# Graph network, edge stage: single node rows fetched by SyncE and ScalarE, and store addresses loaded in pairs

## The reference, cut to what matters

```python
N, C, E = 12500, 64, 412500              # nodes, channels, edges (sorted by dst)
def message_layer(x, e, nvec, src, dst):
    x_send, x_recv = x[src], x[dst]      # one row of the node table for each edge
    flux_send = einsum('ecd,ed->ec', mlp_flux(x_send).reshape(E, C, 2), nvec)
    flux_recv = einsum('ecd,ed->ec', mlp_flux(x_recv).reshape(E, C, 2), nvec)
    a_ws = mlp_a((x_send + x_recv) * 0.5)         # 3 hidden layers of 64, layer norm
    flux = 0.5 * (flux_send + flux_recv) - 0.5 * a_ws * (x_send - x_recv)
    return x + segment_sum(flux, dst, N)
x = layernorm(x + three_mean_aggregations(x, src, dst))
return layernorm(x + message_layer(x, edge_attr_64, edge_attr_2, src, dst))
```

## Time and profile before

| | |
|---|---|
| three runs, median | 7139.81 us (7138.31 to 7141.95) |
| the profiled execution: its time, its span | 7138.85 us, 7137.1 us |
| edge stage: first gather to last | 3056.9 to 7072.0 us |
| busy over the span: PE, DVE, ACT, POOL | 76%, 68%, 37%, 72% |
| gathers of the edge stage | 3199 of 0.951 us, mean |

### The profile page before, as it was taken

The page is one execution under the profiler, slowest core; times in us unless marked ns, Lnnn a source line. Parts: engine busy times, 40 slices in busy tenths (PEclk is TensorE's granted clock), DMA queues, the critical chain, the costliest instruction groups (busy, mean ns, idle before and its releaser), DMA issues.

```text
span 7137.1 us, 176662 instructions
## 1 busy us (share of the span) xinstructions
PE 5406.3 (76%) x49929; PEld 4402.1 (62%) x50131; DVE 4861.2 (68%) x9655; ACT 2628.9 (37%) x5446; POOL 5165.2 (72%) x5041
## 2 busy tenths in 40 slices
PE   2699999999999999946666666666666666666665
PEld 2599999999999999934444444444444444444443
DVE  6899898933223555566777777777777777777776
ACT  0588888920000111123333333333333333333333
POOL 4588887847775777367777777777777777777774
PEclk6799999999999999978888888888888888888887
DMA  5333333446666777656666666666666666666664
GB/s 159 119 139 139 138 138 127 143 169 227 226 227 214 244 238 242 204 153 160 173 166 170 165 170 169 168 168 169 170 165 170 169 171 165 170 166 173 165 170 116
DMA packets 578142, 1230.55 MB, mean 172 GB/s; under 512 B 335288, under 2 KB 416189, under 8 KB 550923
## 3 DMA queue, kind: packets, MB, share of 16 engines
q0 software_dynamic: 211504, 615.59, 32.4%
q1 hardware_dynamic: 316622, 568.88, 24.0%
q10 hardware_dynamic: 49405, 38.76, 1.9%
HBM read 1020.92 MB, written 197.70 MB: 171 GB/s over the span
## 4 chain that ended last, share of the span: by engine, by line
POOL 21%; issue 13%; PE 8%; DMA 6%; SPq 6%; ACT 1%; ACTq 1%; DVE 0%; POOLq 0%; DVEq 0%
POOL edge_rows L1978 21%; DMA edge_rows<-node_table,edge_et 5%; PE edge_mp L2006 4%; SPq L1891 2%; SPq L1888 2%; PE edge_zp L2017 1%; PE edge_tp L1995 1%; SPq L1835 1%; PE edge_tp L1998 1%; ACT edge_h L2082 1%; DMA node_sums<-edge_seg 1%; PE edge_sums_ps L2032 1%; SPq L1923 1%; ACTq L1835 0%; DMA edge_et<-edges_turned 0%
## 5 line engine op out<-in xcount | busy, mean ns | idle before, releaser
L1978 POOL DMA_INDIRECT edge_rows<-node_table,edge_et x3199 | 3041.1, 951 | 975.4 <-issue 923.3
L1995 PE MATMUL edge_tp<-ident,edge_yc 128*128 128x128 f32 x1612 | 539.7, 354 | 1384.2 <-ACT edge_h L2082 1344.5
L1386 PE MATMUL two_acc<-x_parts,win 128*128 128x192 bf16 x16072 | 1387.8, 247 | 17.2 <-issue 11.2
L874 POOL DMA_INDIRECT two_rows<-x_parts,src_at x1120 | 1063.8, 950 | 449.7 <-issue 340.0
L1386 PEld LDWEIGHTS two_acc<-x_parts,win 128*128 128x128 fp8e4 x16072 | 1344.2, 98 | 28.8 <-issue 18.2
L2074 ACT ACTIVATE edge_yc<-edge_rows 128x512 f32<-128x512 f32 x403 | 253.7, 630 | 2571.6 <-DMA edge_rows<-node_table,edge_et 2521.5
L1995 PEld LDWEIGHTS edge_tp<-ident,edge_yc 128*128 128x128 f32 x1612 | 283.9, 176 | 1474.9 <-issue 1407.9
L2006 PE MATMUL edge_mp<-edge_h,edge_W 128*128 128x512 f32 x1612 | 1159.8, 860 | 8.9 <-ACT edge_h L2082 8.9
L1106 ACT ACTIVATE win<-one_count 128x784 fp8e4<-128x784 f32 x1312 | 1071.2, 825 | 144.6 <-PE one_count L1057 80.9
L874 POOL DMA_INDIRECT one_rows<-x_parts,src_at x560 | 862.4, 1540 | 181.7 <-issue 169.4
L2221 DVE TENSOR_REDUCE edge_ssq<-edge_sq 128x8 f32<-128x512 f32 x403 | 276.3, 686 | 959.7 <-ACT edge_sq L2089 953.8
(11 more groups left out here) (334 smaller groups left out, 7475.5 us busy)
## 6 DMA issues: line engine op xcount, KB each, us to landing
win<-adjacency SPq DMA_DIRECT2D x80, 3136.0 KB
adjacency<-win SPq DMA_DIRECT2D x41, 3136.0 KB
edge_near<-near_ids SPq DMA_DIRECT2D x101, 768.0 KB
edge_lone_rows<-node_table SPq DMA_DIRECT2D x3200, 1.3 KB
edge_rows<-node_table,edge_et POOLq DMA_INDIRECT x3199
two_rows<-x_parts,src_at POOLq DMA_INDIRECT x1120
node_table<-two_row SPq DMA_DIRECT2D x49, 322.0 KB
edge_own<-node_table SPq DMA_DIRECT2D x46, 322.0 KB
```

The lines of the kernel that those rows point to most:

```text
L874: pool.indirect_dma_start(rows[:, b % ring, e, :], None, XP.rearrange("p (j c) -> (p j) c", c=3 * C), bass.IndirectOffsetOnAxis(ap=src_at[ ...
L1386: mm = pe.matmul(acc[b][:, half * 3 * C:(half + 1) * 3 * C], win[:, b, half, j, :].bitcast(FP8), now[:, j, :], start=(j == 0), stop=(j == ...
L1978: pool.indirect_dma_start(rows[:, h.b, t, :], None, T5, bass.IndirectOffsetOnAxis(ap=et[:, h.b, 0, t:t + 1].bitcast(I32), axis=0))\
L1995: pe.matmul(to, yc[:, h.b % 2, 2 * pr:2 * pr + 2, :].rearrange("p t c -> p (t c)"), ident[:, :], is_transpose=True, start=True, stop=False)
```

## The change

SP fetches a lone tile in every eight steps instead of every sixteen: tile 0 of the steps 10, 18, ... 402, 50 in all (`LONES`). ACT fetches one more in every sixteen steps: tile 0 of the steps 62, 78, ... 398, 22 in all (`ACT_LONES`); it issues 8 rows in each of ten steps and 12 in each of the four after them, and does none in the two left (`ACT_FETCHED`). SP issues 20 rows in four steps and 16 in three (`LONE_FETCHED`), places its own tile in the eighth step, and places ACT's in the fourth step of every second round.

The row addresses are made at the stage's start: SP loads the source numbers of all these tiles, DVE multiplies them by the bytes of a row, SP writes them to a scratch tensor `LONE`, and a tile's list is read from there. Registers are then loaded without a check of bounds (`several`), and the DMA uses the loaded byte address as it is (`fetch_rows`). SP loads the addresses of the `y_parts` windows eight at once, for four steps; ACT loads the two store addresses of a step at once. ACT's loop body becomes sixteen steps long instead of eight.

```diff
-LONE = 2 * RB
-LONE_AT = (HS - 1) % LONE
-LONE_FIRST = LONE_AT + LONE
-LONE_QUEUES = 4
+LONE_AT = (HS - 1) % RB
+LONE_FIRST = LONE_AT + RB
+LONES = (HS - LONE_FIRST + RB - 1) // RB
+LONE_QUEUES = 8
+PEEL = DONE_PEEL + 2 * RB
+ACT_FROM, ACT_TURNS, ACT_AHEAD = DONE_PEEL + RB, 14, 19
+ACT_TARGET = ACT_FROM + ACT_AHEAD
+ACT_LONES = (HS - RB - ACT_FROM) // (2 * RB)
+ACT_FETCHED = tuple(8 * k + 4 * max(0, k - 10) for k in range(ACT_TURNS + 1))
+LONE_FETCHED = (0, 20, 40, 60, 80, 96, 112, P)
...
+        def several(engine, a, most, why):
+            return nc.values_load_multi_w_load_instructions(a, engines=(engine,), min_val=0, max_val=most, skip_runtime_bounds_check_because=why)[1]
+
+        def fetch_rows(eng, engine, mine, at, to, signals):
+
+            begins = several(engine, at[0:1, mine.start:mine.stop], (N - 1) * 4 * W5, "node numbers of the edges' sources")
+            table = T5.rearrange("n c -> (n c)").bitcast(U8)
+            for i, begin in zip(mine, begins):
+                eng.dma_start(row_bytes(to[i:i + 1, :]), table[bass.ds(begin, 4 * W5)].rearrange("(o a c) -> o a c", o=1, a=2))\
+                    .then_inc(signals[i % LONE_QUEUES], 16)
+
+        def store(eng, h, u, at=None):
...
+            at = base_of(eng, 2 * h.c + u) if at is None else at
...
+            sp.wait_ge(lone_scaled, 2)
+            sp.dma_start(LONE[0:LONES, :], lone_bytes[:, :]).then_inc(lone_listed, 16)
+            sp.dma_start(LONE[LONES:LONES + ACT_LONES, :], act_bytes[:, :]).then_inc(lone_listed, 16)
...
-                sp.dma_start(lone_ids[:, :], src[bass.ds((h.c + LONE - 1) * HE, P)].rearrange("(o e) -> o e", o=1)).then_inc(lone_ids_in, 16)
+                sp.dma_start(lone_at[:, :], LONE[bass.ds(n, 1), :]).then_inc(lone_at_in, 16)
...
+                    bases[:] = several(mybir.EngineType.SP, base_i[0:1, bass.ds(2 * h.c, RB)], N - 1, "bases are held at or under the last node")
...
+                if h.place == ACT_TARGET:
+                    place_rows(h, h.twice, act_in, act_rows, act_placed)
-            double_turns(sp, step, HS, DONE_PEEL + 2 * RB)
+            double_turns(sp, step, HS, PEEL)
...
-                lone = h.place % LONE == LONE_AT and not early(h, LONE_FIRST)
-                for t in range(1 if lone else 0, TL):
+                lone, apart = h.place % RB == LONE_AT and not early(h, LONE_FIRST), h.place == ACT_TARGET
+                for t in range(1 if lone or apart else 0, TL):
...
+                    if apart and t == TL - 1:
+                        pool.wait_ge(act_placed, 16 * (h.twice + 2))
+                        pool.sem_inc(sems["issued"], 1)
...
+            def fetch_own(h):
+                turn = h.place - ACT_FROM - 1
...
+                if turn == 0:
+                    act.wait_ge(act_at_in, 16 * (h.twice + 1))
...
+                    act.wait_ge(act_placed, 16 * (h.twice + 1))
...
+                fetch_rows(act, mybir.EngineType.Activation, range(ACT_FETCHED[turn], ACT_FETCHED[turn + 1]), act_at, act_rows, act_in)
...
                 done_root(h)
+                list_rows(h)
+                fetch_own(h)
...
-            chunks(act, step, HS - RB, RB, DONE_LAG)
+            double_turns(act, step, HS - RB, ACT_FROM)
...
+            dve.wait_ge(lone_src_in, 64)
+            dve.tensor_scalar(act_bytes[:, :], act_src[:, :], float(4 * W5), None, ALU.mult).then_inc(lone_scaled, 1)
+            dve.tensor_scalar(lone_bytes[:, :], lone_src[:, :], float(4 * W5), None, ALU.mult).then_inc(lone_scaled, 1)
```

More of the change, by code:

```diff
@@ L1873, in list_lone @@
             def list_lone(h):
[L1875 removed]
+                n = lone_number(h)
+                if early(h, LONE_AT + 2):
+                    sp.wait_ge(lone_listed, 32)
+                    sp.sem_inc(sems["storing"], 1)
+                sp.dma_start(lone_at[:, :], LONE[bass.ds(n, 1), :]).then_inc(lone_at_in, 16)
             def fetch_lone(h, turn):
@@ L1885, in fetch_lone, with place_rows @@
                         sp.sem_inc(sems["storing"], 1)
[L1886 to L1896, removed]
+                fetch_rows(sp, mybir.EngineType.SP, range(LONE_FETCHED[turn], LONE_FETCHED[turn + 1]), lone_at, lone_rows, lone_in)
+            def place_rows(h, n, arrived, fetched_rows, placed):
                 for q in range(LONE_QUEUES):
-                    sp.wait_ge(lone_in[q], 16 * P // LONE_QUEUES * (n + 1))
+                    sp.wait_ge(arrived[q], 16 * P // LONE_QUEUES * (n + 1))
                     sp.sem_inc(sems["storing"], 1)
@@ L1908, in step @@
                     sp.sem_inc(sems["storing"], 1)
-                if lone_turn == 0 and not early(h, LONE_AT + 1):
+                if turn_of_lone == 0 and not early(h, LONE_AT + 1):
                     list_lone(h)
@@ L1921, in step @@
                                  NEAR16[bass.ds(h.c * HE, 4 * HE)].partition_broadcast(WK)).then_inc(near_in[h.b // 4], 16)
+                    bases[:] = several(mybir.EngineType.SP, base_i[0:1, bass.ds(2 * h.c, RB)], N - 1, "bases are held at or under the last node")
+                at_turn = 2 * (h.place % 4)
+                if h.place == PEEL and at_turn:
+                    bases[at_turn:] = several(mybir.EngineType.SP, base_i[0:1, bass.ds(2 * h.c, RB - at_turn)], N - 1, "bases are held at or under the last node")
                 for u in range(2):
-                    sp.dma_start(yd[:, h.b % 4, u, C:2 * C], Y3[bass.ds(base_of(sp, 2 * h.c + u) * 3, WK), :]).then_inc(yd_in[h.b % 4], 16)
+                    own_base = bases[at_turn + u]
+                    sp.dma_start(yd[:, h.b % 4, u, C:2 * C], Y3[bass.ds(own_base * 3, WK), :]).then_inc(yd_in[h.b % 4], 16)
                 if not early(h, DONE_PEEL):
@@ L2106, in take, with list_rows @@
                 act.activation(seg[:, h.b, :], fold_ps, ACT.Copy).then_inc(sems["seg_out"], 1)
+            def list_rows(h):
+                if h.place == ACT_FROM:
+                    act.wait_ge(lone_listed, 32)
+                    act.dma_start(act_at[:, :], LONE[bass.ds(LONES + h.twice, 1), :]).then_inc(act_at_in, 16)
+            def fetch_own(h):
+                turn = h.place - ACT_FROM - 1
+                if turn < 0 or turn >= ACT_TURNS:
+                    return
+                if turn == 0:
+                    act.wait_ge(act_at_in, 16 * (h.twice + 1))
+                    act.sem_inc(sems["issued"], 1)
+                    act.wait_ge(act_placed, 16 * (h.twice + 1))
+                    act.sem_inc(sems["issued"], 1)
+                fetch_rows(act, mybir.EngineType.Activation, range(ACT_FETCHED[turn], ACT_FETCHED[turn + 1]), act_at, act_rows, act_in)
             def step(h):
+                ats = None
                 if not early(h, ACT_BACK):
-                    store(act, h.back(ACT_BACK), 0)
+                    ats = several(mybir.EngineType.Activation, base_i[0:1, bass.ds(2 * h.back(ACT_BACK).c, 2)], N - 1, "bases are held at or under the last node")
+                    store(act, h.back(ACT_BACK), 0, ats[0])
                 take_y(h)
@@ L2115, in step @@
                 if not early(h, ACT_BACK):
-                    store(act, h.back(ACT_BACK), 1)
+                    store(act, h.back(ACT_BACK), 1, ats[1])
                 for k, run in stages[3:]:
```

53 lines of the change are left out of this document (35 added, 18 removed).

## The result

The changed kernel takes 7105.35 us in the median (7091.37 to 7109.55), the kernel before in the same comparison 7140.88. The ratio is 0.9947 with an interval of 0.9931 to 0.9963: 35.5 us faster, where 60 were forecast, and outside the forecast range. The profiled execution took 7109.55 us, its span 7107.8. It is the slowest of four (7091.37, 7104.17, 7106.53, 7109.55), so what is lost differs from one execution to the next, and what follows is read from one trace of each kernel.

A forecast was written before the change was run, and what follows sets the result against it. POOL's gathers, 1.2555 us each without waits, were taken to bound the kernel; 47 fewer gave 7138.85 - 59.0 = 7079.8 us, plus 0.96 to the median, so 7081, with work added elsewhere hidden; range 7074 to 7098.

The forecast's parts named there:

- POOL's pace, 47 x 1.2555 = 59.0 us: Edge stage on POOL: 47 gathers fewer, each taking its 1.2555 us interval with it, save 59.0 us.
- SP: right in its sum: SP's work in sixteen steps: 142 us, bounds 124 to 160, against 156.9 that they will last.
- Its lead: SP's `edge_et` issue: some 3 us late after two steps, then recovered, staying at least 8 us ahead of POOL's step.
- ACT: the step that failed: ACT's added rows and load: 3.3 us for eight, 4.9 for twelve, fitting about 5.7 us idle a step.
- Nothing is queued between them and `take_y` but the first store: ACT's step: only that store lies between row fetches and `take_y`, so 8-row steps fit and 12-row ones overrun up to 1 us.
- counts for nothing: ACT's second store: its address load, which goes, lay beside ReLUs, so removing it was priced at nothing.
- A microsecond for at most four steps, with two idle steps behind them, is covered: ACT's 12-row steps: lateness absorbed by 7.8 us in hand before POOL; uncovered it would cost up to 88 us.
- Stores behind rows: ACT's queue: stores wait for earlier landings; if that held `take_y` every step, it would be part of the same 7.8 us.
- The second case: Rival: ACT and rows late on 88 12-row steps, part of the gain given back, 7107 us (7090 to 7125); chance 0.12.
- The third: Rival: SP and ACT hold up each other's DMA issues, making the kernel slower, about 7400 us; chance 0.05.
- the fourth: Rival: no change, as SP sets the pace with rows at 0.41 us, 160 us for sixteen steps; chance 0.05.
- The rule on one-row transfers: DMA queues: one engine would carry all 384 rows, 30.7 us in 156.9, about 0.84 busy; sum unchanged, landings may lengthen.

The follow-up runs named there:

- late_store_et: The change with ACT's second store behind all activations and SP's rows spread 12, 16, 20, 20, 20, 20, 20: 7084.83 us, 0.9929 of the kernel before.
- all_three: The change with eight store addresses loaded at once, the second store behind the activations and SP's rows spread 12, 16, 20, ...: 7086.92 us, 0.9930 of before.
- no_act: The change without ACT's tile fetches, POOL gathering those 22 tiles again: 7109.72 us, 0.9960 of the kernel before.
- late_store: The change with ACT's second store issued behind all activations of the step, not in the middle: 7108.61 us, 0.9961 of the kernel before.
- later_only: The change with ACT's same 14 turns of 8 and 12 rows, each one step later: 7091.35 us, 0.9934 of the kernel before.
- et_shift: The change with only SP's rows spread 12, 16, 20, 20, 20, 20, 20 over its seven steps: 7088.17 us, 0.9930 of before.
- base_once: The change with ACT loading eight store addresses at once in every fourth step: 7088.66 us, 0.9931 of the kernel before.

## Why the prediction was wrong

- **POOL's pace, 47 x 1.2555 = 59.0 us: right, where POOL doesn't wait.** The profiled execution of `late_store_et`, the fastest of its four, took 7080.89 us, 58.0 under that of before, at 1.2548 us a gather. Medians of the variants with at most one stall and no wait for the copy to speak of are 52 to 54 us under before. In the trace of `all_three`, whose span is 5.4 us over the sum, 3.9 lie between the gathers and 1.9 behind the last; why is open.
- **SP: right in its sum.** 20 rows in 6.80 us are (6.80 - 0.23) / 19 = 0.346 us a row (0.34 taken). From window to window SP's sixteen steps, each by its median, add up to 158.0 us, of which 9.0 are waits for sums, so at most 149 of work (142 taken, 124 to 160 as bounds). **Its lead was wrongly taken to stay:** at the steps that are 4 modulo 16 `edge_et` was issued 14.7 us ahead of POOL before (that is the median, too), 6.3 in the change, where at least 8 was forecast, and 13.7 in `no_act`, which has nearly all of SP's added work. SP's place is not free: the copy two steps earlier holds it to PE's sums, so lateness of ACT comes out as a late `edge_et`:

```profile
5938.41 0.62 SPq L1953 DMA_DIRECT2D edge_et<-edges_turned  x1
...
5944.60 0.94 POOL L2023 DMA_INDIRECT edge_rows<-node_table,edge_et  x1 [1.51 <-DMA edge_et<-edges_turned]
```

- **ACT: the step that failed.** Rows and their load are as forecast: 0.56 + 2.80 = 3.4 us for eight (3.3), 0.79 + 4.23 = 5.0 for twelve (4.9; 4.23 is such a turn at 4435). But "Nothing is queued between them and `take_y` but the first store" left out a wait that the diff shows, turn 0's for `act_placed`, with the rows, the store and `take_y` behind it. And the paired address load was costed at what goes, not at what comes: "counts for nothing" was 0.697 - 0.278 = 0.42 us in each step, 6.7 in sixteen. An account of sixteen steps, of some 16 x 5.7 = 91 us idle: rows and loads 10 x 3.4 + 4 x 5.0 = 54, addresses 6.7, the mid-step wait 316.6 / 21.3 = 14.9 (3370 us are 21.3 rounds), the copy 63.1 / 21 = 3.0, in all 79. A term that the sum lacked comes on top: a step's rows landed (the last update of `gathered` for it, steps 60 to 393) 2.06 us in the median after the end of its last gather in the kernel before and 2.62 in the change, 9 us in sixteen steps. The mean still fits, but only just: ACT waited 489.8 / 21.3 / 16 = 1.4 us a step for rows, where about 3 were forecast. The step with the copy doesn't fit (14.3 us from `take_y` to `take_y` on average, 10 for POOL), nor does what follows four long turns.
- **"A microsecond for at most four steps, with two idle steps behind them, is covered": wrong.** Over the steps from 18 on the margin from PE's sums to POOL was 10.0 us in the median before, 6.1 after, and at the 18 stalls for sums it was used up. The two steps behind the long turns are not both idle: in the first ACT's loop ends and begins again, 2.8 us (median) without an instruction. Turn 0 and its wait come right behind them. In 10 of 20 rounds ACT was waiting for rows again by then, as in the stall above; in the others the rows lay there already.
- **Stores behind rows: seen as possible, priced at nothing.** `take_y` waited for them 42 times, 227.3 us, in the change (18.2 before), and the wait in mid-step, 316.6 us, was not in the prediction. Taking the latter away won nothing by itself (`late_store`).
- **The rivals.** The second case had the right sign and size (7107), but its mechanism, long steps alone, was the smaller part: 7 of 21 stalls. The third and the fourth did not come. Against the third, SP's rows in the change stood 0.334 us apart on average where ACT issued rows beside them and 0.335 where it didn't; against the fourth stand SP's 9.0 us of waits in sixteen steps.
- **The rule on one-row transfers** (the Trainium skill, DMA: Bandwidth & Descriptors, "Why a DMA increments its semaphore by 16 and not by 1"): in the trace a row is one packet of 1288 bytes and 0.056 us (0.08 was taken) and one of 4 bytes, so each is one engine's work, as the page has it; which engine's, no run shows. With all 384 rows in sixteen steps and no stall POOL begins a gather every 1.2548 to 1.2568 us, so its pace doesn't show them. The landings do, and the prediction drew that from the rule: 2.06 us (median) from the end of a step's last gather to its landing before, 2.15 with SP's rows alone (`no_act`), 2.42 to 2.65 in all kernels in which ACT fetches rows too, those without stalls among them. Whether one hot engine does that or the sixteen together, whose share went from 0.64 to 0.66, no run tells.

## What to carry to other kernels

An engine with idle time is not free for a wait. When work is moved to it, write down each semaphore that the new code waits on, who sets it, and what stands ahead of that in the setter's own queue; add these to the price of the work, for the worst step and not for the mean. If two in-order engines wait on each other once in a round, moving either's part in that wait by a step or by a dozen rows can be worth as much as cutting its work: `later_only` and `et_shift` took 7091.35 and 7088.17 us, `base_once` 7088.66.

## What the hardware showed unexpectedly

A load of registers isn't priced by its count. On ACT one store address took 0.29 us, two at once 0.70, eight 0.74; of a list of rows eight numbers took 0.56, twelve 0.79, and ten 1.01 from a start of 0 or 20 but 2.20 from 10 or 30. Loads of rows that started at a multiple of four numbers and held a multiple of four took 0.06 to 0.09 us a number in all runs, on ACT and on SP, and the dearest of the others 0.22. The start is not all of it: in `base_once` the same loads of eight took 0.72 from most starts, and in `no_act` the two store addresses took 0.50. What makes a load dear was not tried by itself.
